# A batched attention and gated FFN layer on one core: a second buffer for the gated product, smaller units of work, and the order of an iteration as one table

## The chip, the cores and the metric

One core of a Trainium2 chip runs the whole kernel. The metric is the device time of one execution in microseconds. The engines are PE (TensorE: matmuls, with its weight loads shown apart as PEld), ACT (ScalarE), DVE (VectorE), POOL (GpSimd) and SP, which here only issues DMAs. Each engine works through its own list of instructions in order; semaphores tie the lists together.

## The reference

For 16 sequences x of 512 tokens and 256 channels (all fp32):

```
x  = layernorm(x + attention(x))          # 16 heads of 16, causal softmax, bqkv and bout
h  = silu(x W1 * s1) * (x W2 * s2)        # 256 -> 1024, gate and up
h  = gelu(h H1 * sh1); h = gelu(h H2 * sh2)   # 1024 -> 1024, twice, exact gelu
out = layernorm(x + (h W3) * s3)          # 1024 -> 256
```

## The kernel before, in words

**Stages.** Sequences are pipelined over 19 iterations (-1 to 17). Iteration i computes the attention of sequence i, prepares that of i+1, and does the feed-forward part of sequence i-1 and what is left of i-2. Each step in the list of an iteration carries that offset (0, 1, -1, -2). Iterations 3 to 14 run in a loop of two and hold every step; the first and the last iterations hold only those whose sequence exists. All engines walk the same list of steps and do their own part of each step, so the order of the list is the order of every engine's work. `plan_iteration` writes it: four blocks of exponentials (one for each group of four heads), each followed by one hidden layer over 256 tokens (a half) of the feed-forward part, whose eight column blocks are its units.

**Attention.** For key block kt (of 128) of a group, `exp` makes the scores of a pair of heads on PE into one of two PSUM banks `pS` (L834, L840), ACT takes the exponential into `probs_a` or `probs_b` (L530, L541), POOL masks the diagonal block of each pair (L488), and `pv` multiplies with the values (L873). ACT instructions per group: 4 + 4 single heads for kt 0 and 1, 2 pairs for kt 2, one of all four heads for kt 3, 11 in all. In the list one `exp` step stands for a pair of heads. `max` makes the row maxima of the group to come, two heads to a step (PE L851 into two banks `pM`, DVE L674), `neg_max` turns and stores them (DVE L682 and L684, PE L859, ACT L546, four DMAs of SP L416). `qk` projects queries and keys (PE L882, ACT `c_hi` L551, DVE `c_lo` L689), then SP saves them with five DMAs (L394).

**Feed-forward.** Operands are split into a high and a low part, so every product takes two matmuls. One `gu` unit is eight matmuls of 256 columns (L923), then

```
ACT  th[j%2] = tanh(gate)            L586
DVE  th[j%2] = (th[j%2] + 1) * up    L703
DVE  th[j%2] = gate * s2 * th[j%2]   L706
ACT  Xhi[j]  = th[j%2]               L592   (step ffn_hi)
POOL Xlo[j]  = th[j%2] - Xhi[j]      L494   (step ffn_hi)
```

The two buffers of `th` are held until POOL has read them: the tanh of unit j waits for the Xlo of unit j-2. The hidden layers take 16 matmuls per unit (L937); ACT writes the high part and the full value (L609, L610), DVE the low part (L714). The first unit of layer h1 waits for seven of the eight Xlo before its first matmul, for the eighth before its last pair. `ffn_out` (L950) and `y` (L904) are steps of both 128-token tiles of a half.

**Shared memory.** qk, v, gu, h1, h2, ffn_out, y, x1_turn, neg_max and den_turn share three PSUM banks in turn (`ring`); a step waits until the last user of its bank has been read. `th` lies over `Osb`, the attention's output row, so the ACT copy L571 waits for the feed-forward half before. A `table` step makes ACT load the table of Exp or Gelu (L597).

Of the kernel before, what the change touches and what calls it, by code (L numbers as in the profile page):

```python
# [55 lines left out]

def plan_iteration():

    steps = []

    def add(kind, off, *args):
        steps.append((kind, off, args))

    def exps(g, between):

        e = 0
        for kt in range(TB):  # L70
            for p in range(PAIRS):
                add("exp", 0, g, kt, p)
                steps.extend(between.get(e, []))
                e += 1
            if kt:
                add("pv", 0, g, kt - 1)

    def last_pv(g):
        add("pv", 0, g, TB - 1)
        add("o_out", 0, g)  # L80
        add("stack", 0 if g + 2 < NG else 1, (g + 2) % NG)

    def hidden(layer, off, half, g, early, after):

        if not early:
            last_pv(g)
            steps.extend(after.get(-1, []))
        for j in range(early, KB):  # L90
            add(layer, off, half, j)
            waiting = [(layer, half, k) for k in range(early)] if j == early else []
            for k, unit in enumerate(waiting):
                steps.append(("h_act", off, unit))
                if k == 0:
                    last_pv(g)
            if waiting:
                steps.append(("h_rest", off, waiting.pop(0)))
            add("h_act", off, layer, half, j)
            steps.extend(after.get(j, []))  # L100
            steps.extend(("h_rest", off, unit) for unit in waiting)
            add("h_rest", off, layer, half, j)

    def maxes(off, g):
        return [("max", off, (g, t, p)) for t in reversed(range(TB)) for p in range(PAIRS)]

    def gated(off, half, at, others):

        between = {e: list(more) for e, more in others.items()}
        for e, n in at:  # L110
            between.setdefault(e, []).append(("gu", off, (half, n)))
            if n:
                between.setdefault(e + (e == 6 and n == KB - 1), []).append(("ffn_hi", off, (half, n - 1)))
        return between


    m = maxes(0, 1)
    add("table", 0, "Exp", 0)
    exps(0, {0: [("y", -1, (0,)), m[0]], 1: [("y", -1, (1,))], 2: [("h2", -2, (1, 0))],
             4: [m[1]], 5: [m[2]], 6: [("h2", -2, (1, 1))], 7: [("ln1_stats", -1, ()), m[3]]})  # L120
    add("table", 0, "Gelu", 1)
    hidden("h2", -2, 1, 0, 2, {2: [m[4]], 3: [m[5]], 4: [m[6]], 5: [m[7]], 6: [("neg_max", 0, (1,))]})
    add("table", 0, "Exp", 2)
    add("ffn_out", -2, 1)
    m = maxes(0, 2)
    add("ln1", -1)

    exps(1, gated(-1, 0, [(4, 0), (4, 1), (5, 2), (5, 3), (6, 4), (6, 5), (7, 6), (7, 7)],
                  {0: [("qk", 0, (3,)), ("load_xT", 1, ()), m[0]], 1: [("x1_turn", -1, (0,))],
                   2: [("x1_turn", -1, (1,))], 3: [m[1]], 5: [m[2]]}))  # L130
    steps.append(m[3])
    add("ffn_hi", -1, 0, KB - 1)
    add("table", 0, "Gelu", 3)
    hidden("h1", -1, 0, 1, 0, {0: [m[4]], 1: [m[5]], 2: [m[6]], 3: [m[7]],
                               4: [("neg_max", 0, (2,))], 5: [("ln2_stats", -2, (1,))], 6: [("ln2", -2, (1,))]})

    m = maxes(0, 3)
    add("table", 0, "Exp", 4)
    add("qk", 1, 0)
    exps(2, {0: [("h2", -1, (0, 0))], 1: [m[0]], 2: [("h2", -1, (0, 1))], 3: [m[1]], 4: [m[2]], 6: [m[3]]})  # L140
    add("table", 0, "Gelu", 5)
    hidden("h2", -1, 0, 2, 2, {2: [m[4], ("load_x", 0, ())], 3: [m[5]], 4: [m[6]], 5: [m[7]], 6: [("neg_max", 0, (3,))]})
    add("table", 0, "Exp", 6)
    add("qk", 1, 1)
    add("ffn_out", -1, 0)
    m = maxes(1, 0)

    add("gu", -1, 1, 0)
    exps(3, gated(-1, 1, [(0, 1), (1, 2), (2, 3), (3, 4), (4, 5), (5, 6), (6, 7)],
                  {1: [m[0]]}))  # L150
    steps.append(m[1])
    add("ffn_hi", -1, 1, KB - 1)
    add("table", 0, "Gelu", 7)
    hidden("h1", -1, 1, 3, 0, {-1: [("v", 1, (0,)), m[2]], 0: [m[3], ("v", 1, (1,)), ("den", 0, ())],
                               1: [m[4], ("v", 1, (2,))], 2: [m[5], ("v", 1, (3,))], 3: [m[6], ("rec_save", 0, ())],
                               4: [m[7], ("rec_load", 0, ())], 5: [("neg_max", 1, (0,)), ("qk", 1, (2,))],
                               6: [("ln2_stats", -1, (0,)), ("den_turn", 0, ())], 7: [("ln2", -1, (0,))]})
    return steps
# [866 lines left out]
```

## Time and profile before

| | before |
|---|---|
| median of 3 runs | 2489.56 us (2488.16 to 2493.21) |
| the profiled execution: its time | 2490.49 us |
| its span, first to last instruction | 2488.7 us |
| PE busy | 2284.1 us, 92% |
| ACT busy, DVE busy | 1308.9 us, 1274.0 us |
| mean granted clock of PE | 0.961 |
| iterations -1 and 0 | from 18.2 to 194.2 us |
| iterations 1, 2 | start at 194.2, 334.4 us |
| iterations 3 to 14 | 478.8 to 2208.7 us, 144.2 us each |
| iterations 15, 16, 17 | start at 2208.7, 2346.9, 2462.3 us |

How to read it: an iteration starts with the first matmul of its first `exp` step (L834). A matmul's record holds its passage through the array as well, so records of matmuls that follow each other overlap; idle time is counted only where no record runs. "[0.54 <-DVE mx L674]" behind a row says that the engine was idle for 0.54 us before it and what ended the wait.

### The profile page before, as it was taken

The page shows a single profiled execution, that of the slowest core. Times are in us where ns is not written, and L with a number is a line of the kernel's source. Part 1 is how long each engine was busy: PE and PEld are TensorE (multiplying, and loading weights), DVE is VectorE, ACT ScalarE, POOL GpSimd, SP SyncE. Part 2 cuts the span into 40 slices and gives each one's busy share as a digit, 9 for nine tenths or more (in the row PEclk, how much of TensorE's full clock was granted, in tenths as well). Part 3 has the DMA queues.
Part 4 walks back from the last instruction along what each step waited for, and adds up shares of the span by engine and source line. Part 5 has one row for each costly group of instructions (what it writes and reads, how often), then busy time and mean ns, then how long its engine had stood idle before and what let it go on. Part 6 is the DMA issues. An engine that isn't in the chain of part 4 may idle for free. (4 is left out here: it accounts for less than half of the span.)

```text
span 2488.7 us, 51639 instructions
## 1 busy us (share of the span) xinstructions
PE 2284.1 (92%) x16294; PEld 1888.8 (76%) x16294; DVE 1274.0 (51%) x3963; ACT 1308.9 (53%) x2784; POOL 478.9 (19%) x894
## 2 busy tenths in 40 slices
PE   4566999999999999999999999999999999999987
PEld 2224888788788877878887787878778787887887
DVE  3364455555555455555545555554555555555433
ACT  1324555555565555556555555655555565655533
POOL 0112212212221221222122122211222121212211
PEclk8667999999999999999999999999999999999989
DMA  4851222122122212212221222222122222221000
GB/s 140 287 200 54 73 65 81 53 78 70 55 78 79 69 51 77 78 53 73 78 76 45 76 81 61 72 69 78 50 68 81 61 78 61 78 60 39 20 5 9
DMA packets 110394, 184.04 MB, mean 74 GB/s; under 512 B 21632, under 2 KB 39808, under 8 KB 109952
## 3 DMA queue, kind: packets, MB, share of 16 engines
q1 hardware_dynamic: 110128, 180.70, 25.3%
q8 instruction: 142, 2.33, 0.4%
q14 instruction: 124, 1.02, 0.1%
HBM read 109.86 MB, written 72.88 MB: 73 GB/s over the span
## 5 line engine op out<-in xcount | busy, mean ns | idle before, releaser
L674 DVE CUSTOM_DVE_ANT_0 pM<-pM,mask 128x512 f32<-128x512 f32 (+3 forms) x1024 | 490.4, 510 | 417.8 <-PE pM L851 340.7
L937 PE MATMUL ring<-Xhi,H 128*128 128x256 f32 x2048 | 538.3, 300 | 49.6 <-POOL Xlo L494 41.9
L937 PE MATMUL ring<-Xlo,H 128*128 128x256 f32 x2048 | 516.7, 289 | 0.0
L937 PE MATMUL ring<-Yhi,H 128*128 128x256 f32 x2048 | 509.2, 287 | 0.0
L937 PE MATMUL ring<-Ylo,H 128*128 128x256 f32 x2048 | 500.2, 282 | 0.0
L937 PEld LDWEIGHTS ring<-Xhi,H 128*128 128x128 f32 x2048 | 405.2, 198 | 65.9 <-POOL Xlo L494 30.0
L937 PEld LDWEIGHTS ring<-Xlo,H 128*128 128x128 f32 x2048 | 406.2, 198 | 4.4 <-issue 3.3
L937 PEld LDWEIGHTS ring<-Yhi,H 128*128 128x128 f32 x2048 | 390.6, 191 | 21.9 <-issue 21.2
L937 PEld LDWEIGHTS ring<-Ylo,H 128*128 128x128 f32 x2048 | 391.4, 191 | 0.7
L851 PE MATMUL pM<-Ks,Qs 128*128 128x512 f32 (+3 forms) x1024 | 285.8, 356 | 36.2 <-DVE mx L674 24.0
L609 ACT ACTIVATE Yhi<-ring,cols 128x256 fp32r<-128x256 f32 x256 | 121.6, 475 | 348.2 <-PE ring L937 309.8
L923 PE MATMUL ring<-x1Thi,W 128*128 128x256 f32 x1024 | 259.5, 288 | 9.2 <-DVE th L706 7.7
L851 PEld LDWEIGHTS pM<-Ks,Qs 128*128 128x128 f32 x1024 | 178.2, 196 | 105.5 <-DVE mx L674 58.2
L923 PE MATMUL ring<-x1Tlo,W 128*128 128x256 f32 x1024 | 254.2, 283 | 0.0
L488 POOL TENSOR_SCALAR_AFFINE_SELECT probs_a<-probs_a 128x256 f32<-128x256 f32 x256 | 104.3, 407 | 776.2 <-ACT probs_a L530 702.3
L610 ACT ACTIVATE full_h<-ring,cols 128x256 f32<-128x256 f32 x512 | 239.0, 467 | 0.0
L834 PE MATMUL pS<-Qs,Ks 128*128 128x512 f32 (+1 forms) x512 | 191.3, 431 | 39.5 <-DMA Qs<-nm 24.8
L494 POOL TENSOR_TENSOR Xlo<-th,Xhi 128x256 fp32r<-128x256 f32 x256 | 186.9, 733 | 210.1 <-ACT Xhi L592 210.1
L714 DVE TENSOR_TENSOR Xlo<-full_h,Xhi 128x256 fp32r<-128x256 f32 x256 | 109.7, 429 | 219.9 <-ACT full_h L610 217.4
L923 PEld LDWEIGHTS ring<-x1Thi,W 128*128 128x128 f32 x1024 | 195.2, 191 | 33.9 <-issue 17.3
L586 ACT ACTIVATE th<-ring,cols 128x256 f32<-128x256 f32 x256 | 121.6, 475 | 185.5 <-POOL Xlo L494 94.1
L609 ACT ACTIVATE Xhi<-ring,cols 128x256 fp32r<-128x256 f32 x256 | 120.7, 472 | 171.3 <-PE ring L937 123.3
(97 smaller groups left out, 3456.1 us busy)
## 6 DMA issues: line engine op xcount, KB each, us to landing
Qs<-qk_d SPq DMA_DIRECT2D x128, 256.0 KB, 3.9
Ks<-qk_d SPq DMA_DIRECT2D x64, 512.0 KB, 4.9
qk_d<-c_hi SPq DMA_DIRECT2D x64, 256.0 KB, 2.4
qk_d<-c_hi SPq DMA_DIRECT2D x128, 128.0 KB, 2.4
qk_d<-c_lo SPq DMA_DIRECT2D x128, 128.0 KB, 2.4
xTs<-in_xT SPq DMA_DIRECT2D x16, 512.0 KB, 4.0
Oc<-Osb SPq DMA_DIRECT2D x256, 32.0 KB
H<-raw SPq DMA_DIRECT2D x8, 1024.0 KB, 10.4
```

Of the source, the lines that this page charges most:

```text
L488: nc.gpsimd.affine_select(out=tri_p, in_=tri_p, compare_op=ALU.is_ge, fill=0.0, base=0, pattern=[[0, 2], [1, P]], channel_multiplier=-1).t ...
L494: nc.gpsimd.tensor_tensor(Xlo[:, j], th[:, j % 2], Xhi[:, j].bitcast(F32), ALU.subtract).then_inc(x_lo, 1)
L586: nc.scalar.activation(th[:, j % 2], ring[:, BANKS[kind, off, a], 0:HALF], ACT.Tanh, scale=s1_c[:, j:j + 1]).then_inc(tanh_done, 1)
L609: nc.scalar.activation(hi, src, ACT.Gelu, scale=sc)
L610: nc.scalar.activation(full_h[:], src, ACT.Gelu, scale=sc).then_inc(h_full, 1)
L674: nc.vector.tensor_tensor_reduce(pM[:, s, 0:n], pM[:, s, 0:n], mask[:, T - n:T], 1.0, NEG, ALU.add, ALU.max, mx[:, t, 2 * p + s:2 * p + s ...
L714: nc.vector.tensor_tensor(lo, full_h[:], hi.bitcast(F32), ALU.subtract).then_inc(h_lo, 1)
L834: nc.tensor.matmul(pS[:, u % 2, 0:n], keys[p], Qs[:, slot, p, s, kt * P:T], start=True, stop=True).then_inc(e_ready, 1)
L851: nc.tensor.matmul(pM[:, s, 0:n], Qs[:, slot, p, s, t * P:(t + 1) * P], Ks[:, slot, p, 0:n], start=True, stop=True).then_inc(m_ready, 1)
L923: mm = nc.tensor.matmul(to[:, n * HALF:(n + 1) * HALF], w, x_part, start=(c == 0 and X is x1Thi), stop=(c == CB - 1 and X is x1Tlo))
L937: mm = nc.tensor.matmul(to, w, x_part, start=(k == 0 and m == 0), stop=(k == KB - 1 and m == 1))
```

## The change

1. The second DVE operation of a gated unit writes a new pair of buffers, `full_g`, which ACT's copy and POOL's subtraction then read. `th` is free again when DVE has read it. `full_g` is laid over `c_hi`, the buffer of the qk step, and this brings two waits: DVE's second operation of the first unit of each half waits until SP's saves of the qk step before it have landed (`qk_saved`), and ACT's `c_hi` waits for the Xlo of the gated units before it.
2. Steps get smaller: one `exp` step is one of the 11 exponentials, one `max` step one head, a unit of h1 or h2 two steps of 8 matmuls each, `y` and `ffn_out` one tile each. The instructions stay the same in number and size.
3. The waits of PE for the low parts get finer: the first h1 or h2 unit starts when four of eight are there, then asks for six, seven and eight; `ffn_out` asks for all but four, then for all but one, then all.
4. `plan_iteration` reads the order from a table. In it, units 0 and 1 of the next group's exponentials stand before more other work, maxima stand apart, `ln1` stands before `ffn_out`, one `v` step before the last two `pv` of group 3, `qk:1:2` after the last h1 unit instead of before the seventh.

The table for the stretches that the prediction speaks of (a word is kind:offset:arguments), and the core of the rest:

```diff
+exp:0:0:0 exp:0:0:1
+
+table:0:Exp:0 y:-1:0:0 y:-1:0:1 max:0:1:3:0 y:-1:1:0 max:0:1:3:1 exp:0:0:2 exp:0:0:3 h2:-2:1:0:0 y:-1:1:1
+exp:0:0:4 exp:0:0:5 h2:-2:1:0:1 exp:0:0:6 exp:0:0:7 pv:0:0:0 exp:0:0:8 max:0:1:3:2 max:0:1:3:3 exp:0:0:9
+h2:-2:1:1:0 exp:0:0:10 max:0:1:2:0 h2:-2:1:1:1 max:0:1:2:1 pv:0:0:1 ln1_stats:-1 max:0:1:2:2 max:0:1:2:3
...
+table:0:Exp:2 ln1:-1 ffn_out:-2:1:0 ffn_out:-2:1:1 exp:0:1:0 exp:0:1:1 qk:0:3 load_xT:1 max:0:2:3:0 exp:0:1:2
+max:0:2:3:1 exp:0:1:3 x1_turn:-1:0 exp:0:1:4 x1_turn:-1:1 exp:0:1:5 pv:0:1:0 exp:0:1:6 exp:0:1:7 max:0:2:3:2
+max:0:2:3:3 gu:-1:0:0 gu:-1:0:1 ffn_hi:-1:0:0 exp:0:1:8 exp:0:1:9 max:0:2:2:0 gu:-1:0:2 ffn_hi:-1:0:1
+gu:-1:0:3 ffn_hi:-1:0:2 ffn_hi:-1:0:3 gu:-1:0:4 max:0:2:2:1 gu:-1:0:5 ffn_hi:-1:0:4 pv:0:1:1 exp:0:1:10
+gu:-1:0:6 ffn_hi:-1:0:5 gu:-1:0:7 ffn_hi:-1:0:6 pv:0:1:2 max:0:2:2:2 max:0:2:2:3 ffn_hi:-1:0:7
+
+table:0:Gelu:3 pv:0:1:3 o_out:0:1 stack:0:3 h1:-1:0:0:0 h1:-1:0:0:1 h_act:-1:h1:0:0 max:0:2:1:0 max:0:2:1:1
...
+h_rest:-1:h2:0:7 qk:1:1
+
+table:0:Exp:6 ffn_out:-1:0:0 ffn_out:-1:0:1 gu:-1:1:0 exp:0:3:0 exp:0:3:1 gu:-1:1:1 ffn_hi:-1:1:0 exp:0:3:2
...
+ffn_hi:-1:1:5 gu:-1:1:7 ffn_hi:-1:1:6 pv:0:3:1 exp:0:3:10 max:1:0:3:2 max:1:0:3:3 ffn_hi:-1:1:7 v:1:0 pv:0:3:2
+
+table:0:Gelu:7 pv:0:3:3 o_out:0:3 stack:1:1 max:1:0:2:0 max:1:0:2:1 h1:-1:1:0:0 h1:-1:1:0:1 h_act:-1:h1:1:0
...
+h_act:-1:h1:1:6 den_turn:0 h_rest:-1:h1:1:6 ln2_stats:-1:0 h1:-1:1:7:0 h_act:-1:h1:1:7 h_rest:-1:h1:1:7
+h1:-1:1:7:1 ln2:-1:0 qk:1:2
...
+        c_at = nc.sbuf_base
         c_hi = sb("c_hi", [P, T], F32R)
+        full_g = over(nc, c_at, "full_g", [P, 2, HALF], F32)
...
-                        nc.gpsimd.tensor_tensor(Xlo[:, j], th[:, j % 2], Xhi[:, j].bitcast(F32),
+                        nc.gpsimd.tensor_tensor(Xlo[:, j], full_g[:, j % 2], Xhi[:, j].bitcast(F32),
...
                         need(act, qk_saved, (b * NG + g) * SAVES)
+                        need(act, x_lo, (b - off - 1) * (2 * KB) + gated_before(g))
...
-                            need(act, x_lo, (b - 1) * (2 * KB) + (g + 1) // 2 * KB)
+                            need(act, ffn_full, (b - 1) * (2 * KB) + (g + 1) // 2 * KB)
...
-                        need(act, x_lo, b * (2 * KB) + n - 1)
+                        need(act, ffn_full, b * (2 * KB) + n - 1)
...
-                        nc.scalar.activation(Xhi[:, j], th[:, j % 2], ACT.Copy).then_inc(x_hi, 1)
+                        nc.scalar.activation(Xhi[:, j], full_g[:, j % 2], ACT.Copy).then_inc(x_hi, 1)
...
-                        nc.vector.scalar_tensor_tensor(out=th[:, j % 2], in0=gate,
+                        if j == 0:
+                            saved = (b + 2) * NG + qk_before(half)
+                            dve.wait_ge(qk_saved, (min(saved, B * NG) if isinstance(b, int) else saved) * SAVES)
+                        need(dve, x_lo, n - 1)
+                        nc.vector.scalar_tensor_tensor(out=full_g[:, j % 2], in0=gate,
...
-                        for k in range(KB):
-                            if j == 0 and k in (0, KB - 1):
-                                pe.wait_ge(s, n - (k == 0))
+                        for k in range(part * KB // 2, (part + 1) * KB // 2):
+                            if j == 0 and k in (0, KB // 2, KB - 2, KB - 1):
+                                pe.wait_ge(s, n - {0: 4, 4: 2, 6: 1, 7: 0}[k])
```

## Rows read from the trace of the kernel before

**Rows 1.** Part 1 of the page: busy time of each engine, share of the span.
```profile
PE 2284.1 (92%) x16294; PEld 1888.8 (76%) x16294; DVE 1274.0 (51%) x3963; ACT 1308.9 (53%) x2784; POOL 478.9 (19%) x894
```
**Rows 2.** Windows, one per iteration; length, busy of each engine, clock, DMA.
```profile
622.10:765.00 142.90, 137.96 (x1020) 115.34 (x1019) 77.07 (x247) 81.55 (x174) 29.57 (x55) 1.00 0.25 70
...
1198.70:1344.20 145.50, 140.55 (x1020) 117.94 (x1019) 77.09 (x247) 81.59 (x174) 29.55 (x55) 0.98 0.24 68
...
sum 1729.90, PE 1669.40 PEld 1396.94 DVE 925.73 ACT 978.95 POOL 354.73; mean PE 139.12 PEld 116.41 DVE 77.14 ACT 81.58 POOL 29.56
```
**Rows 3.** Window of iteration 8 behind the longest wait of PE.
```profile
1252.70:1259.50 6.80, 5.87 (x27) 5.87 (x28) 2.91 (x11) 3.29 (x7) 1.46 (x2) 0.50 0.09 19
```
**Rows 4.** Waits of the whole span: us in total, times, longest.
```profile
ACT th L586 <- POOL Xlo L494: 94.1, 141, 0.9
...
PEld pS L840 <- ACT probs_b L530: 54.1, 63, 1.4
PE ring L937 <- POOL Xlo L494: 41.9, 18, 4.0
```
**Rows 5.** Timeline of the gated stretch of iteration 8, ACT, DVE and POOL.
```profile
1250.32 0.47 ACT L586 ACTIVATE th<-ring,cols 128x256 f32<-128x256 f32 x1 [0.42 <-POOL Xlo L494]
...
1252.00 0.47 ACT L586 ACTIVATE th<-ring,cols 128x256 f32<-128x256 f32 x1 [0.90 <-POOL Xlo L494]
...
1252.96 0.48 DVE L706 SCALAR_TENSOR_TENSOR th<-ring,cols,th 128x256 f32<-128x256 f32 x1
...
1253.48 0.42 ACT L592 ACTIVATE Xhi<-th 128x256 fp32r<-128x256 f32 x1 [0.70 <-DVE th L706]
...
1253.97 0.73 POOL L494 TENSOR_TENSOR Xlo<-th,Xhi 128x256 fp32r<-128x256 f32 x1 [0.40 <-ACT Xhi L592]
```
**Rows 6.** Timeline of PE, same stretch: waits, and two neighbouring matmuls.
```profile
1248.44 0.39 PE L923 MATMUL ring<-x1Thi,W 128*128 128x256 f32 x1 [0.22 <-DVE th L706]
...
1250.99 0.41 PE L873 MATMUL pO<-probs_b,Vo 128*17 128x128 f32 x8 [0.24 <-POOL probs_b L488]
1253.63 0.58 PE L937 MATMUL ring<-Xhi,H 128*128 128x256 f32 x1 [2.22 <-POOL Xlo L494]
...
1260.74 0.28 PE L937 MATMUL ring<-Xlo,H 128*128 128x256 f32 x1
1260.86 0.28 PE L937 MATMUL ring<-Xhi,H 128*128 128x256 f32 x1
```
**Rows 7.** Timeline of PE in groups 0 and 3 of iteration 8.
```profile
1201.77 0.98 PE L834 MATMUL pS<-Qs,Ks 128*128 128x512 f32 x2 [0.26 <-ACT probs_a L530]
1202.59 1.89 PE L904 MATMUL ring<-Wout,Oc 128*128 128x256 f32 x8
...
1209.75 0.44 PE L851 MATMUL pM<-Ks,Qs 128*128 128x384 f32 x1 [0.54 <-DVE mx L674]
1210.39 0.44 PE L851 MATMUL pM<-Ks,Qs 128*128 128x384 f32 x1 [0.21 <-DVE mx L674]
...
1320.13 0.41 PE L873 MATMUL pO<-probs_b,Vo 128*17 128x128 f32 x8 [0.82 <-POOL probs_b L488]
```
**Rows 8.** Chain of waits: a gated unit, a hidden unit, one behind a pv.
```profile
2251.14 0.96 PE ring L923 x8
...
2296.24 2.10 PE ring L937 x16
2299.12 1.91 PE ring L937 x16
```
**Rows 9.** SP's queue in iteration 8: the first and last saves of a qk step.
```profile
1303.15 0.90 SPq L394 DMA_DIRECT2D qk_d<-c_hi  x2
...
1305.37 0.60 SPq L394 DMA_DIRECT2D qk_d<-c_hi  x1
```
**Rows 10.** Part 6 of the page: a save's time from issue to landing.
```profile
qk_d<-c_hi SPq DMA_DIRECT2D x64, 256.0 KB, 2.4
```
**Rows 11.** Windows of the two gated stretches of iteration 16.
```profile
2376.00:2394.93 18.93, 13.53 (x81) 12.83 (x81) 7.25 (x16) 6.36 (x16) 5.82 (x8) 0.77 0.00 1
2428.11:2445.74 17.63, 12.06 (x83) 11.36 (x82) 8.68 (x19) 6.47 (x16) 5.81 (x8) 0.85 0.00 1
```

More of the change, by code:

```diff
@@ L54 @@
 MISC = 3
-def plan_iteration():
[L62 to L158, printed above, removed]
@@ new lines, with value @@
+h_rest:-1:h1:1:3 h1:-1:1:4:0 h1:-1:1:4:1 h_act:-1:h1:1:4 max:1:0:0:2 max:1:0:0:3 rec_load:0 h_rest:-1:h1:1:4
+h1:-1:1:5:0 h1:-1:1:5:1 h_act:-1:h1:1:5 neg_split:1:0 neg_max:1:0 h_rest:-1:h1:1:5 h1:-1:1:6:0 h1:-1:1:6:1
+h_act:-1:h1:1:6 den_turn:0 h_rest:-1:h1:1:6 ln2_stats:-1:0 h1:-1:1:7:0 h_act:-1:h1:1:7 h_rest:-1:h1:1:7
+h1:-1:1:7:1 ln2:-1:0 qk:1:2
+"""
+def plan_iteration():
+    def value(word):
+        return int(word) if word.lstrip("-").isdigit() else word
+    steps = [[value(w) for w in entry.split(":")] for entry in ORDER.split()]
+    return [(s[0], s[1], tuple(s[2:])) for s in steps]
@@ L161, with bank_of @@
 STEPS = plan_iteration()
-BANKED = [s for s in STEPS if s[0] in
-          ("qk", "v", "gu", "h1", "h2", "ffn_out", "y", "x1_turn", "neg_max")]
+PARTED = {"h1": 2, "h2": 2, "ffn_out": 1, "y": 1}
+def bank_of(kind, off, args):
+    return (kind, off, args[:PARTED[kind]]) if kind in PARTED else (kind, off, args)
 def ring_banks():
@@ L170, in ring_banks, with qk_before, gated_before @@
     for kind, off, args in STEPS:
-        n = 2 if kind == "den_turn" else 1 if (kind, off, args) in BANKED else 0
-        for m in range(n):
-            key = (kind, off, args + (m,)) if kind == "den_turn" else (kind, off, args)
-            banks[key] = at % MISC
-            at += 1
+        if kind == "den_turn":
+            keys = [(kind, off, (m,)) for m in range(CB)]
+        elif kind in ("qk", "v", "gu", "x1_turn", "neg_max") or kind in PARTED:
+            keys = [bank_of(kind, off, args)]
+        else:
+            keys = []
+        for key in keys:
+            if key not in banks:
+                banks[key] = at % MISC
+                at += 1
     return banks
 BANKS = ring_banks()
+def qk_before(half):
+    first = next(n for n, s in enumerate(STEPS) if s[0] == "gu" and s[2][0] == half)
+    return sum(s[0] == "qk" for s in STEPS[:first]) - sum(s[0] == "qk" and s[1] == 0 for s in STEPS)
+def gated_before(g):
+    at = next(n for n, s in enumerate(STEPS) if s[0] == "qk" and s[2] == (g,))
+    return sum(s[0] == "ffn_hi" for s in STEPS[:at])
 def steps_of(i):
@@ L727, in work @@
                                                     ALU.mult).then_inc(o_norm, 1)
-                    elif kind == "y":
-                        half, = a
+                    elif kind == "y" and a[1]:
+                        half, _ = a
                         xr = xz[:, (odd + off) % 2]
@@ L754, in work @@
                         row.then_inc(ln1, 1)
-                    elif kind == "ffn_out":
-                        half, = a
+                    elif kind == "ffn_out" and a[1]:
+                        half, _ = a
                         at = b * LN2 + 6 * half
-                        f = ring[:, BANKS[kind, off, a]].rearrange("p (t c) -> p t c", c=C)
+                        f = ring[:, BANKS[bank_of(kind, off, a)]].rearrange("p (t c) -> p t c", c=C)
                         two = xz[:, (odd + off) % 2, 2 * half:2 * half + 2]
@@ L806, in iteration, with bank @@
             def iteration(i, steps, odd, taken, general):
-                def bank(kind, off, a):
+                def bank(kind, off, a, first=True):
                     n = BANKS[kind, off, a]
+                    if not first:
+                        return ring[:, n]
                     if n in taken:
@@ new lines, in iteration @@
+                        for p in sorted({p for p, _ in heads}):
+                            wide = [k for k, (m, _) in enumerate(heads) if m == p]
+                            first, last = heads[wide[0]][1], heads[wide[-1]][1]
+                            mm = nc.tensor.matmul(pS[:, nth % 2, n * wide[0]:n * (wide[-1] + 1)],
+                                                  Ks[:, slot, p, kt * P:(kt + 1) * P],
+                                                  Qs[:, slot, p, first:last + 1, kt * P:T], start=True, stop=True)
```

191 lines of the change are left out of this document (105 added, 86 removed).

## The prediction

> **What bounds the kernel now.** I read the page's busy times, then the windows by iteration, the waits, and the timeline of one iteration. PE is busy 92% of the span and no other engine over 53% [rows 1], so the time is PE's work, plus what PE waits, plus what its clock takes. The twelve full iterations take 1729.9 us, 144.2 each [rows 2]. The view has twelve such rows: six at granted clock 1.00 with a mean length of 143.1 us (622.10:765.00 stands for them), six at 0.98 or 0.99 and up to 145.9 (1198.70:1344.20 stands for them). So about 1.0 us an iteration is lost to the clock. In iteration 8 all of it lies in one stretch at 0.50, the lower of its two levels, and that stretch begins inside PE's longest wait [rows 3, 6].
>
> In iteration 8 PE sits idle for 145.5 - 140.55 = 4.95 us [rows 2]. That is a lower bound of its waits: a matmul's record lasts 0.28 us where the next one starts 0.12 us later [rows 6], so each wait hides 0.16 us or more under the record before it. There are some fifteen such places, so the waits come to 5.0 + 15 x 0.16 = 7.4 us. Starts against starts of unhindered steps of the same kind (a gated unit 0.96, a hidden unit 1.91 [rows 8]) give about the same, 7.5. The rest, 135.6 us, is work that the change keeps.
>
> Where they are. (A) The gated stretch of group 1, before h1: 0.22 + 0.24 + 2.22 us idle [rows 6], 3.3 with what is hidden. The cause is a loop across three engines: ACT's list has tanh(j), then the copy of unit j-1; POOL subtracts; then only is `th` free for tanh(j+1). Tanh starts are 1252.00 - 1250.32 = 1.68 us apart [rows 5], against PE's 0.96 [rows 8]; ACT waits so 141 times, 94.1 us [rows 4]. PE's units pile up behind it and h1 waits for the last low parts. (B) The last `pv` of group 3: 0.82 idle [rows 7], 1.0 in all; its mask stands behind late subtractions on POOL. (C) The exponentials of group 0: 0.26 + 0.54 + 0.21 idle [rows 7], 1.7 in all; a pair of heads is asked for while ACT and DVE have just begun the pair before. (D) The same in groups 1 to 3, seen only in the weight loads (54.1 us for one form [rows 4]), some 1.6 us an iteration.
>
> **The change, part by part.**
> *Two more buffers.* `th` is now held from the tanh to the end of DVE's second operation, 1252.96 + 0.48 - 1252.00 = 1.44 us; `full_g` from 1252.96 to POOL's end at 1253.97 + 0.73, 1.74 us [rows 5]. With two of each that is 0.72 and 0.87 us a unit, under PE's 0.96. PE sets the pace again. The last unit's chain from its tanh to Xlo stays: 1253.97 + 0.73 - 1252.00 = 2.7 us [rows 5]. After the last gated unit (1248.44 + 0.96 + its wait, so 1249.6) PE has a `pv`, two maxima and a `pv`, which end at 1250.99 + 0.41 [rows 6], 1.8 us with their wait and 1.4 without, and now also seven eighths of the first h1 unit, 1.7 [rows 8]: 3.1 us against 2.7 and ACT's queue of two or three instructions in front of that chain. I leave 0.7 us of wait of the 3.3: A gives 2.6.
> *B.* The exponential of kt 3 stands before two maxima, the `v` step and a `pv`, and POOL no longer lags: 1.0 gained. `v` before the last two `pv` makes ACT's copy to `Vo` wait for the last `pv`, with the table load and the output copy queued behind it; the h1 unit in between (1.9 us [rows 8]) covers them, so nothing. Without that cover it would cost about 1.3.
> *Single exp and max steps.* They cost no instruction. In group 0 there now stand three of the four tiles of `y` and two maxima between exponentials 1 and 2; two tiles last 1.89 us with their passage [rows 7], so some 2.5 us, in which ACT gets through both. I take 1.6 of C's 1.7. For D, I take 0.7 of 1.6: in groups 1 and 3 ACT has exponentials, tanh and copies together, and its in-order queue will still make PE wait.
> *Half units.* The cost of a split is bounded by 0 and by the difference of two hidden units, 2.10 behind a `pv` against 1.91 [rows 8]; I take 0, as no fp32 step stands between most halves. Three such neighbourhoods vanish (two pairs of `pv` become adjacent, `v` joins them) and `y` adds one: two times 0.19, 0.3 gained.
> *`ln1` before `ffn_out`* on DVE fills time in which it waited for PE: nothing alone, it is in D. *`qk:1:2` behind the last h1 unit* puts ACT's c_hi before the exponentials of group 0; exponential 2 has the 2.5 us of cover above: nothing. ACT's new wait of c_hi for the Xlo: h1 has used them all by then, nothing. ACT's copy to `Osb` now waits for DVE instead of POOL, which comes earlier: nothing. SP's list keeps its DMAs and nearly its order, with the saves of `qk:1:2` a unit later; nobody waits for these before the next block.
> *New waits.* DVE's second operation of a half's first unit waits for the saves. From the first issue at 1303.15 to the last at about 1305.4, and 2.4 us to land [rows 9, 10]: 4.6 us behind c_lo. In half 1, `ffn_out` (32 matmuls at 0.12, 3.8 us) and the first gated unit stand between, so the saves land at about the same moment as they are asked for; in half 0 it is six exponentials, both `x1_turn`, a `pv`, two maxima and a gated unit, an estimated 5 us or more. Bounds: 0, and two waits of 1.5. Behind that operation stand DVE's maxima and the release of the gated unit's bank, so PE would feel it one to one. I take 0.2 an iteration, and 0.4 for finer handoffs that don't fit.
> Sum of waits: 2.6 + 1.0 + 1.6 + 0.7 + 0.3 - 0.6 = 5.6 us. *Clock:* the fall follows the 2.22 us wait; with 0.7 left I expect it to go, 1.0 us. Together 6.6 us an iteration.
>
> The clock is the place where I weigh a rule. The rows show one fall, right at the one long wait [rows 3, 6], but six iterations with the same wait have none [rows 2]. The Trainium skill, page "TensorE: Matmul & The Clock Gate", section "A second HAM failure mode: psum-queue depth-cycling", says that many small idle moments between groups of matmuls while cycling through PSUM banks can make the gate go up and down. By it the falls would stay, as small waits stay, and the sum would be 5.6.
>
> **Outside the loop.** Iteration 1 lacks some steps: 5 us. Iterations 2 to 15 as above: 14 x 6.6 = 92. In iteration 16 the gated stretches up to the end of the first h1 unit take 18.9 and 17.6 us [rows 11]. Now: eight units (7.7, and an estimated 1.9 more in the first at the low clock that shows in the 0.77), 2.7 of chain, 0.3 of last matmuls: 12.6 and 10.7. That is 6.3 + 6.9, and an estimated 1.8 of low clock behind them: 15 us. Up to 194 us DMAs and weight tests rule; 0, within 5 either way. Sum: 5 + 92 + 15 = 112. The profiled execution took 2490.5 us, 0.9 over the median; 2490.5 - 112 - 0.9 = 2377.
>
> **The rivals.**
> 1. *The waits go elsewhere.* With the `th` loop gone, ACT (81.6 of 144 us busy, crowded in the gated blocks) or the three ring banks bind, or the falls of the clock stay. For it: D's waits, and the rule above. Against: ACT's pitch there is 0.8 us a unit by its two durations less their overlap [rows 5]. Only A and the tail: 15 x 2.6 + 15 = 54, 2436; falls alone staying, 2377 + 14 = 2391.
> 2. *More than I give.* All 7.5 and the clock: 15 x 8.8 + 18 = 150, 2340.
> 3. *Slower: the saves bind.* Place: the second operation of the first unit of each half, behind SP's queue [rows 9, 10]. SP issues in order; if a transfer with a wait stood ahead of the saves, they'd come late. The point from which it decides is where the two waits together pass 6.6 us an iteration, that is landings 8 us behind c_lo instead of 4.6. At 9 us: 2 x 4.3 = 8.6 lost, net 2.0 x 15 - 15 = 15 us slower, 2505. Against: the steps that SP has ahead are done long before in this trace.
> 4. *The table does not change PE's order much*, since PE's records show 92% busy: within 0.2% (about 5 us, what a measurement can tell from no change). Against: the 94.1 us of ACT's waits [rows 4].
>
> **How the numbers follow.** Forecast, 2355 to 2405 (the falls staying included): 0.58. Rival 1 beyond that: 0.25. Rival 2: 0.11. Rival 3: 0.04. Rival 4: 0.02. Faster by over 0.2% then 0.94, same 0.02, slower 0.04. The range runs from rival 2's value to just short of rival 1's, 2342 to 2430, with about 2 in 10 left outside.
>
> **What would show it.** Right: ACT th waiting for DVE th or PE and no more for POOL; tanh starts about 1.0 us apart in iteration 16; PE's wait before h1 under 0.8 us and POOL probs_b gone from PE's waits; windows of 137 to 138 us at clock 1.00. Wrong: windows above 140 us; DVE's second gated operation idle behind SP's saves; PE's waits for ACT probs_a or probs_b grown; falls to 0.50 in the same place with no long wait ahead.

## The result, and the profile after

The changed kernel takes 2341.3 us (median of 4 runs, 2337.4 to 2344.8) where the kernel before takes 2491.3 on the same chip: ratio 0.940, 95% interval 0.938 to 0.942. I had said 2377. The side and the mechanisms were right, the size was not: 150 us came off, 112 were forecast, and the result lies just under the range (its lower end is 2342), beside the value of rival 2. The span of the profiled execution went from 2488.7 to 2335.7 us.

Part 1 of the page of the changed kernel, and from part 2 the granted clock in 40 slices:

```profile
PE 2208.9 (95%) x16294; PEld 1869.4 (80%) x16294; DVE 1277.3 (55%) x3963; ACT 1308.2 (56%) x2784; POOL 476.3 (20%) x894
...
PEclk8667999999999999999999999999999999999999
```

The counts are those of [rows 1], and DVE, ACT and POOL do the same work in the same time. Nothing was saved in work: PE is the engine whose time fell, as it waits less. PE's own figure falls too, since a matmul's record that was stretched, by a wait inside a step or by the low clock, is short again.

Windows of two iterations and of the twelve together (3 to 14):

```profile
1001.00:1136.80 135.80, 134.70 (x1021) 115.71 (x1019) 77.37 (x247) 81.50 (x174) 29.47 (x55) 1.00 0.26 73
1136.80:1271.60 134.80, 134.36 (x1019) 115.73 (x1018) 77.32 (x247) 81.49 (x174) 29.37 (x55) 1.00 0.26 73
...
460.60:2082.20 1621.60, 1614.65 (x12219) 1388.93 (x12217) 928.72 (x2953) 977.74 (x2088) 352.60 (x660) 1.00 0.26 73
```

1621.6 / 12 = 135.1 us an iteration against 144.2 [rows 2]. In iteration 8 PE is idle for 134.80 - 134.36 = 0.44 us, where it was 4.95, and the clock is 1.00 in all of them; from 223 us to the last 4 us of this execution it never falls. The 153 us between the two spans divide into: up to iteration 1, 1.6 (forecast 0); iteration 1, 6.9 (forecast 5); iterations 2 to 15, 126.7 or 9.05 each (forecast 92, 6.6 each); iterations 16 and 17, 17.9 (forecast 15). That is 41 us more than the forecast's sum of 112. The medians lie 150 us apart, as the profiled execution of the changed kernel is 3.9 us below its median.

Waits over the whole span; the lines L578, L532, L701 and L929 are L586, L530/L541, L706 and L937 of before:

```profile
ACT th L578 <- PE ring L915: 70.1, 80, 4.0
...
PEld pS L831 <- ACT probs_b L532: 41.0, 53, 0.9
...
DVE full_g L701 <- DMA qk_d<-c_hi: 8.5, 16, 1.1
...
PE ring L929 <- POOL Xlo L490: 1.0, 3, 0.4
```

ACT's 141 waits for POOL before a tanh, 94.1 us [rows 4], are gone: the view has no such row any more, and what ends ACT's wait there is PE. PE's wait before h1 went from 41.9 us [rows 4] to 1.0. DVE's wait for the saves came as forecast, at "about the same moment as they are asked for": 16 times, 0.53 us on average, one an iteration.

The end of the gated stretch of iteration 8, ACT, DVE and POOL, beside [rows 5]:

```profile
1184.77 0.48 ACT L578 ACTIVATE th<-ring,cols 128x256 f32<-128x256 f32 x1
...
1185.78 0.48 DVE L701 SCALAR_TENSOR_TENSOR full_g<-ring,cols,th 128x256 f32<-128x256 f32 x1
...
1186.30 0.42 ACT L584 ACTIVATE Xhi<-full_g 128x256 fp32r<-128x256 f32 x1 [0.58 <-DVE full_g L701]
...
1186.79 0.74 POOL L490 TENSOR_TENSOR Xlo<-full_g,Xhi 128x256 fp32r<-128x256 f32 x1 [0.27 <-ACT Xhi L584]
```

And PE in the same stretch, beside [rows 6] (the last row is the first matmul of the pair that waits for the last Xlo):

```profile
1184.66 0.63 PE L864 MATMUL pO<-probs_a,Vo 128*17 128x256 f32 x8
1185.22 0.61 PE L842 MATMUL pM<-Ks,Qs 128*128 128x384 f32 x2
1185.76 0.41 PE L864 MATMUL pO<-probs_b,Vo 128*17 128x128 f32 x8
1186.11 0.39 PE L929 MATMUL ring<-Xhi,H 128*128 128x256 f32 x1
...
1187.88 0.28 PE L929 MATMUL ring<-Xhi,H 128*128 128x256 f32 x1
```

The chain of the last unit is what I gave it: 1186.79 + 0.74 - 1184.77 = 2.76 us (2.7 forecast). But ACT's queue delays that tanh by 0.1 us at most, as it starts 0.1 us after PE has gone on to the `pv` behind the unit, and its Xlo is there at 1187.53, 0.35 us before the last pair of the h1 unit begins. No row of PE carries a wait. The 2.22 us of [rows 6] are gone entirely.

Iteration 16, where no attention work covers anything: two tanh starts, then the windows that answer to [rows 11].

```profile
2240.61 0.47 ACT L578 ACTIVATE th<-ring,cols 128x256 f32<-128x256 f32 x1 [0.48 <-PE ring L915]
2241.57 0.48 ACT L578 ACTIVATE th<-ring,cols 128x256 f32<-128x256 f32 x1
```

```profile
2238.40:2250.23 11.83, 10.57 (x80) 9.91 (x81) 7.14 (x16) 6.82 (x16) 5.90 (x8) 1.00 0.00 1
2282.87:2294.61 11.74, 10.32 (x83) 9.74 (x81) 8.58 (x19) 6.82 (x16) 5.91 (x8) 1.00 0.01 1
```

Tanh starts are 0.96 us apart, PE's own pace, where the loop across three engines had set 1.68 [rows 5]. The stretches take 11.8 and 11.7 us (forecast 12.6 and 10.7, before 18.9 and 17.6), at clock 1.00 where it was 0.77 and 0.85.

Just ahead of the first of them PE waits for the layernorm `ln1` before it can turn x1. The row of before, then the one that is left:

```profile
2372.62 1.11 PE L912 MATMUL ring<-ident,xz 128*128 128x128 f32 x4 [2.87 <-DVE xz L752]
```

```profile
2236.36 0.63 PE L904 MATMUL ring<-ident,xz 128*128 128x128 f32 x4 [1.24 <-DVE xz L760]
```

With `ln1` before `ffn_out` in the list, DVE writes `xz` while PE still works on `ffn_out`, and the first `x1_turn` (2234.52 us) no longer waits. The second waits 1.24 us for its bank.

### The profile page after: what moved, and what is told of

It reads as the page before. It is cut to its first block and busy times, and to the rows that moved or that the text cites. A ratio compares the mean times of both kernels' runs of the same rounds, so it can differ in the third digit from the quotient of the medians.

```text
span 2335.7 us, 52022 instructions
## 1 busy us (share of the span) xinstructions
PE 2208.9 (95%) x16294; PEld 1869.4 (80%) x16294; DVE 1277.3 (55%) x3963; ACT 1308.2 (56%) x2784; POOL 476.3 (20%) x894
## 5 line engine op out<-in xcount | busy, mean ns | idle before, releaser
L929 PE MATMUL ring<-Xhi,H 128*128 128x256 f32 x2048 | 515.4, 291 | 6.6 <-ACT full_h L602 5.0
L929 PE MATMUL ring<-Yhi,H 128*128 128x256 f32 x2048 | 507.3, 285 | 0.0
L929 PE MATMUL ring<-Ylo,H 128*128 128x256 f32 x2048 | 502.6, 282 | 0.0
L929 PE MATMUL ring<-Xlo,H 128*128 128x256 f32 x2048 | 499.2, 282 | 0.0
L929 PEld LDWEIGHTS ring<-Xhi,H 128*128 128x128 f32 x2048 | 391.0, 191 | 18.7 <-ACT full_h L602 11.7
L929 PEld LDWEIGHTS ring<-Ylo,H 128*128 128x128 f32 x2048 | 390.8, 191 | 3.2
L929 PEld LDWEIGHTS ring<-Xlo,H 128*128 128x128 f32 x2048 | 392.0, 191 | 1.1
L929 PEld LDWEIGHTS ring<-Yhi,H 128*128 128x128 f32 x2048 | 390.2, 191 | 2.6
L842 PE MATMUL pM<-Ks,Qs 128*128 128x512 f32 (+3 forms) x1024 | 302.1, 355 | 32.6 <-DVE mx L665 17.0
L831 PE MATMUL pS<-Qs,Ks 128*128 128x512 f32 (+2 forms) x768 | 267.9, 409 | 31.2 <-DMA Qs<-nm 23.6
L532 ACT ACTIVATE probs_a<-pS 128x512 f32<-128x512 f32 x384 | 210.7, 592 | 106.8 <-PE pS L831 105.1
L831 PEld LDWEIGHTS pS<-Qs,Ks 128*128 128x128 f32 x768 | 137.7, 194 | 138.4 <-issue 47.4
L532 ACT ACTIVATE probs_b<-pS 128x384 f32<-128x384 f32 (+1 forms) x320 | 154.2, 513 | 116.6 <-PE pS L831 74.6
L490 POOL TENSOR_TENSOR Xlo<-full_g,Xhi 128x256 fp32r<-128x256 f32 x256 | 187.8, 736 | 151.2 <-ACT Xhi L584 146.5
```

The lines of the kernel that those rows point to most:

```text
L490: nc.gpsimd.tensor_tensor(Xlo[:, j], full_g[:, j % 2], Xhi[:, j].bitcast(F32), ALU.subtract).then_inc(x_lo, 1)
L532: nc.scalar.activation(dst, src, ACT.Exp, scale=SCALE).then_inc(exp_done, 1)
L831: mm = nc.tensor.matmul(pS[:, nth % 2, n * wide[0]:n * (wide[-1] + 1)], Ks[:, slot, p, kt * P:(kt + 1) * P], Qs[:, slot, p, first:last + 1 ...
L842: nc.tensor.matmul(pM[:, h % 2, 0:n], Qs[:, slot, h // 2, h % 2, t * P:(t + 1) * P], Ks[:, slot, h // 2, 0:n], start=True, stop=True).then ...
L929: mm = nc.tensor.matmul(to, w, x_part, start=(k == 0 and m == 0), stop=(k == KB - 1 and m == 1))
```

## The experiments

"Starts against starts" means here: the time from a step's first matmul to the next step's, less what the same kind of step takes unhindered, summed over an iteration. It holds the waits, what they hide, the clock, and small fixed costs between steps. Per iteration, by halves of the four groups (an Exp block and the Gelu block behind it; before and e1 have `qk:1:2` inside the last, the others at its end, which moves some 0.4 us from there into the first). The level of these figures depends on which step is taken as unhindered; the differences between the rows do not:

```
                 group 0       group 1       group 2       group 3
               Exp0  Gelu1   Exp2  Gelu3   Exp4  Gelu5   Exp6  Gelu7    sum
before         3.46   0.59   3.33   3.74   1.74   0.59   2.70   1.93   18.1
e1_old_order   3.47   0.59   2.56   0.43   1.72   0.58   2.59   1.99   13.9
e2_one_pair    1.57   0.46   2.16   1.92   1.40   0.38   2.46   1.45   11.8
changed        1.57   0.46   2.03   0.43   1.40   0.38   1.35   1.39    9.0
```

Theory 1 was mine: two separate gains, the `th` loop with its fall of the clock, and the order with its small steps. The rivals: that the order alone is small, that the saves of `c_hi` or the finer waits matter, that the half units are only a cost, that the clock does not hang on the long wait.

**e1_old_order: two buffers and the finer waits, in the order of before.** The table is written so that every engine has the old order, pairs of exponentials and maxima and whole units included:

```diff
-table:0:Exp:0 y:-1:0:0 y:-1:0:1 max:0:1:3:0 y:-1:1:0 max:0:1:3:1 exp:0:0:2 exp:0:0:3 h2:-2:1:0:0 y:-1:1:1
+table:0:Exp:0 exp:0:0:0 exp:0:0:1 y:-1:0:0 y:-1:0:1 max:0:1:3:0 max:0:1:3:1 exp:0:0:2 exp:0:0:3 y:-1:1:0
+y:-1:1:1 exp:0:0:4 exp:0:0:5 h2:-2:1:0:0 h2:-2:1:0:1 exp:0:0:6 exp:0:0:7 pv:0:0:0 exp:0:0:8 max:0:1:3:2
...
```

> The changed kernel (two full_g buffers, finer waits for the low parts) with the order of before written in the new table: pairs of exponentials and of maxima, both halves of a hidden unit side by side, qk:1:2 before the seventh h1 unit. Theory 1 (the order and the buffers each remove their own waits, and the clock falls only behind a long wait of PE): the wait before h1 goes, iterations 144.2 - 2.8 - 1.0 = 140.3 us at clock 1.00, total about 2420, ratio 0.971. Theory 2 (falls of the clock come from many small waits, which this order keeps): falls to 0.50 stay, iterations 141.4, total about 2435. Theory 3 (the order does nearly all; the th loop was hidden): total 2470 or more.

2413.0 us, ratio 0.969 (0.968 to 0.971). Window of iterations 3 to 14, and PE's waits in it:

```profile
470.40:2149.90 1679.50, 1653.05 (x12219) 1384.28 (x12218) 925.14 (x2952) 974.06 (x2088) 354.69 (x660) 1.00 0.26 71
```

```profile
PE pM L843 <- DVE mx L666: 9.0, 24, 0.5
PE ring L930 <- ACT full_h L603: 6.5, 12, 0.7
PE pO L865 <- POOL probs_b L485: 6.4, 12, 0.5
PE pS L832 <- ACT probs_a L533: 3.1, 12, 0.3
```

139.96 us an iteration, 4.2 less than before. No row of PE waiting for Xlo is left in these iterations even in the old order, and the falls of the clock are gone with it. Gelu3 gives 3.3 and Exp2 0.8 of the 4.2; 1.0 of that is the clock. So the waits of A came to 3.1 us, of which I had given 2.6. This run has the finer waits as well as the buffers; no run has the finer waits alone in the old order, so how the 3.1 us divide between the two is not shown there.

**e2_one_pair: the new table, `th` written in place as before.**

```diff
-                        nc.vector.scalar_tensor_tensor(out=full_g[:, j % 2], in0=gate,
+                        nc.vector.scalar_tensor_tensor(out=th[:, j % 2], in0=gate,
...
-                        need(act, ffn_full, b * (2 * KB) + n - 1)
+                        need(act, x_lo, b * (2 * KB) + n - 1)
```

> The new table, but the gated product stays in th as before (no full_g, the tanh of unit j waits for the Xlo of unit j-2, no wait for the saves). Theory 1: the loop of 1.68 us a unit is back in both halves, PE waits about 2.5 to 3 us in half 0 and about 1.5 in half 1, and the clock falls again in some iterations: iterations about 140.5 us, total about 2430, ratio 0.976. Theory 3 (the order does nearly all): iterations under 137, total under 2370.

2390.5 us, ratio 0.961 (0.959 to 0.963), 40 us under what my theory gave. The window, and PE's two largest waits in it:

```profile
465.40:2120.50 1655.10, 1627.01 (x12219) 1390.79 (x12217) 928.72 (x2953) 975.83 (x2088) 352.15 (x660) 1.00 0.26 72
```

```profile
PE ring L924 <- POOL Xlo L490: 11.5, 24, 0.6
PE pO L859 <- POOL probs_b L484: 8.6, 12, 0.7
```

137.9 us an iteration. The `th` loop is back, over the whole span:

```profile
ACT th L577 <- POOL Xlo L490: 62.6, 87, 0.9
```

It costs 2.8 us against the changed kernel (Gelu3 1.5, Exp6 1.1), but here it reaches PE as two waits of 0.6 us or less, and the clock does not fall. The finer waits, which this run has too, may have a share in that; it is not shown apart. Buffers and order overlap: one without the other they give 4.2 (e1) and 6.2, together 9.0. The 1.0 of the clock is in both. POOL's late masks (B) also need both changes: 12 waits of `pv` for probs_b are left in e1 (0.5 us each) and in e2 (0.7), none in the changed kernel.

**e3_coarse_waits: the changed kernel with the two waits of before** (seven of eight low parts, then all).

```diff
-                            if j == 0 and k in (0, KB // 2, KB - 2, KB - 1):
-                                pe.wait_ge(s, n - {0: 4, 4: 2, 6: 1, 7: 0}[k])
+                            if j == 0 and k in (0, KB - 1):
+                                pe.wait_ge(s, n - (k == 0))
```

> The changed kernel with the coarse waits for low parts of before (first hidden unit: seven of eight ahead of its first matmul, the eighth ahead of its last pair; ffn_out likewise). Theory 1: the chain behind the last gated unit is 2.7 us and PE has 1.4 us of other work ahead of h1, so without the finer waits h1:0 starts some 0.8 us later in half 0 and little later in half 1; iterations 135.9 to 136.4, total 2353 to 2363, of it up to 2 us in iterations 16 and 17. Rival (the finer waits do nothing, the chain is over in time): total within 3 us of the changed kernel's 2341.

2353.4 us, ratio 0.945 (0.944 to 0.947), 135.7 us an iteration. PE's first wait in iterations 3 to 14:

```profile
PE ring L929 <- POOL Xlo L490: 4.8, 12, 0.4
```

0.4 us once an iteration, 0.47 from start to start. The other 0.14 of the 0.6 us comes in the last Gelu block, where no row shows a wait. So with coarse waits about the 0.7 us that I had left standing of A does appear; the finer waits, with the cover that I had counted (3.1 us, 3.2 measured), take it away.

**e4_over_Yhi: `full_g` laid over `Yhi`**, which is free then, so that neither DVE waits for the saves nor ACT's `c_hi` for Xlo.

```diff
+        y_at = nc.sbuf_base
         Yhi = sb("Yhi", [P, KB, HALF], F32R)
+        full_g = over(nc, y_at, "full_g", [P, 2, HALF], F32)
...
-                        if j == 0:
-                            saved = (b + 2) * NG + qk_before(half)
-                            dve.wait_ge(qk_saved, (min(saved, B * NG) if isinstance(b, int) else saved) * SAVES)
```

> The changed kernel with full_g laid over the first two blocks of Yhi, which are free in the gated stretches, instead of over c_hi: no wait of DVE for SP's saves and none of ACT's c_hi for the Xlo. Theory 1 (the wait for the saves, 0.53 us of DVE idle 16 times in the trace, is off PE's path): total within 3 us of the changed kernel. Rival (PE feels it through the release of the gated unit's bank one to one): 16 x 0.5 = 8 us less, 2333.

2344.6 us, ratio 0.942 (0.941 to 0.944), 3.3 us above the changed kernel's time on another chip, and 135.1 us an iteration, the changed kernel's to 0.05. In the loop the 0.53 us that DVE waits for the saves are on nobody's path. My 0.2 for them was 0, and rival 3 falls. (Outside it, iteration 15 of the profiled execution takes 135.8 us against 129.6; see the last section.)

**e7_whole_units: each second half of an h unit or `y` tile moved right behind the first.** In the table, for the first block:

```diff
-exp:0:0:4 exp:0:0:5 h2:-2:1:0:1 exp:0:0:6 exp:0:0:7 pv:0:0:0 exp:0:0:8 max:0:1:3:2 max:0:1:3:3 exp:0:0:9
...
+h2:-2:1:0:0 h2:-2:1:0:1 exp:0:0:4 exp:0:0:5 exp:0:0:6 exp:0:0:7 pv:0:0:0 exp:0:0:8 max:0:1:3:2 max:0:1:3:3
...
```

> The table of the changed kernel with the second half of each h1 and h2 unit moved right behind the first, and the second tile of y likewise; all else stays. Theory 1 (half units matter only where they stand between exponentials and maxima: some seven places an iteration, each with a handoff to ACT or DVE of 0.3 to 0.6 us no longer covered): 1 to 2 us an iteration more, total 2356 to 2372. Rival (the places don't matter, only how much work stands in a block): within 3 us of 2341.

2374.9 us, ratio 0.954 (0.952 to 0.955): 33 us slower than the changed kernel, more than I had given it. 137.5 us an iteration, with the largest wait

```profile
PE pS L831 <- ACT probs_b L532: 9.7, 24, 0.4
```

where the changed kernel has no such row in these iterations. With the half unit gone from between them, four exponentials stand in a row, and in groups 0 and 2 the seventh comes 0.56 us later, the next two 0.2 and 0.1 more: 1.7 us in all. Two maxima of group 0 and one of the last Gelu block cost the other 0.5. The rejoined tiles of `y` cost nothing: 0.19 us more behind the first, 0.19 less behind exponential 4. So 2.3 of the 4.9 us that order and small steps bring hang on the half units of h1 and h2: they are filler of a fitting size. (The rest of the table was made for them; a table made for whole units might lose less. Not tried.)

**e8_pairs: exponentials and maxima in pairs again.**

```diff
-max:0:2:3:1 exp:0:1:3 x1_turn:-1:0 exp:0:1:4 x1_turn:-1:1 exp:0:1:5 pv:0:1:0 exp:0:1:6 exp:0:1:7 max:0:2:3:2
...
+max:0:2:3:1 exp:0:1:2 exp:0:1:3 x1_turn:-1:0 exp:0:1:4 exp:0:1:5 x1_turn:-1:1 pv:0:1:0 exp:0:1:6 exp:0:1:7
...
```

> The table of the changed kernel with the second exponential of each pair, and the second maximum, moved right behind the first. Most exponentials stand in pairs already, so this moves mostly maxima. Theory 1: two maxima in a row need two free pM banks, and DVE takes 0.85 us for a row of 512; a few places stall by 0.2 to 0.5 us: 0.5 to 1.2 us an iteration, total 2349 to 2359. Rival (maxima are covered anyway): within 3 us of 2341.

2348.2 us, ratio 0.943 (0.942 to 0.945), 135.7 an iteration. The single steps are worth 0.6 us an iteration, the half units four times that.

**e5_long_wait and e6_shorter_wait: a wait of PE made on purpose.** Coarse waits as in e3, and POOL does three more subtractions (one in e6) into `Ylo`, which nobody reads then, before the seventh Xlo of half 0. They add work and leave the output as it is.

```diff
+                        for m in range(3 if half == 0 and j == KB - 2 else 0):
+                            nc.gpsimd.tensor_tensor(Ylo[:, m], full_g[:, j % 2], Xhi[:, j].bitcast(F32), ALU.subtract)
```

> The kernel of the coarse waits with one long wait put back: before the seventh Xlo of half 0, POOL makes three more subtractions of 0.73 us into Ylo, which is free there. PE then waits 0.4 + 2.2 = 2.6 us ahead of the first h1 matmul of half 0 in each iteration, about as in the kernel before (2.2). Theory 1 (a fall of the clock to 0.50 follows a long wait of PE): falls of 3.4 to 7 us appear in about half of the iterations right behind that wait, as before; iterations 135.75 + 2.2 = 137.95 without and up to 140.8 with a fall, total 2353 + 33 + 15 = about 2400. Rival (the falls of before needed the many small waits as well): no fall between 230 us and the last iterations, total about 2386.

2398.9 us, ratio 0.964 (0.962 to 0.966). Two iterations of it, both with this wait (2.46 and 2.48 us), then the 3.4 us behind the second:

```profile
606.40:744.00 137.60, 134.65 (x1019) 115.74 (x1018) 77.26 (x247) 81.62 (x174) 31.46 (x58) 1.00 0.26 72
744.00:883.80 139.80, 136.31 (x1021) 117.25 (x1019) 77.37 (x247) 81.68 (x174) 31.46 (x58) 0.99 0.26 71
...
796.70:800.10 3.40, 3.40 (x19) 3.40 (x18) 0.28 (x1) 0.66 (x2) 0.03 (x1) 0.50 0.18 40
```

```profile
658.27 0.39 PE L931 MATMUL ring<-Xhi,H 128*128 128x256 f32 x1 [2.46 <-POOL Xlo L492]
...
796.09 0.39 PE L931 MATMUL ring<-Xhi,H 128*128 128x256 f32 x1 [2.48 <-POOL Xlo L492]
```

The falls are back, behind PE's long wait as in [rows 3], in 8 of the 12 iterations. These are 139.0 to 139.7 us long, against 137.6 of those with the same wait and no fall: 1.3 to 2.1 us each.

> As the run with the long wait, with one more subtraction of 0.73 us instead of three: PE waits 0.4 + 0.7 = 1.1 us ahead of h1 of half 0. Theory 1 (it takes a wait of about 2 us or more, since 0.96 us in the run with one pair of buffers had no fall in the full iterations): no fall in iterations 3 to 14, iterations 135.75 + 0.7 = 136.5, total about 2365. Rival (falls grow in number with the wait): some falls in these iterations, and up to 2372.

2366.4 us (one run, beside 2486.9 for the kernel before). The window and the wait:

```profile
465.00:2102.50 1637.50, 1616.07 (x12218) 1388.97 (x12217) 927.80 (x2953) 979.79 (x2088) 361.56 (x672) 1.00 0.26 73
```

```profile
PE ring L931 <- POOL Xlo L492: 13.1, 12, 1.1
```

Twelve waits of 1.1 us and not one fall. No run has a wait between 1.1 and 2.2 us in its loop (for iterations 15 and 16 see the last section), and nothing tells why of two iterations with the same wait one has the fall.

**e9_neighbours: like beside like.** Two `v` steps put behind two others, `pv:0:1:2` beside `pv:0:1:3`, to see whether the fixed 0.19 us behind such a step can be shared.

```diff
-gu:-1:0:6 ffn_hi:-1:0:5 gu:-1:0:7 ffn_hi:-1:0:6 pv:0:1:2 max:0:2:2:2 max:0:2:2:3 ffn_hi:-1:0:7
+gu:-1:0:6 ffn_hi:-1:0:5 gu:-1:0:7 ffn_hi:-1:0:6 max:0:2:2:2 max:0:2:2:3 ffn_hi:-1:0:7 pv:0:1:2
...
-max:1:0:2:2 max:1:0:2:3 v:1:1 den:0 h_rest:-1:h1:1:0 h1:-1:1:1:0 max:1:0:1:0 max:1:0:1:1 v:1:2
+max:1:0:2:2 max:1:0:2:3 den:0 h_rest:-1:h1:1:0 h1:-1:1:1:0 max:1:0:1:0 max:1:0:1:1 v:1:2 v:1:3
```

> The table of the changed kernel with three fp32 steps moved beside others of the kind: v:1:1 behind v:1:0, v:1:3 behind v:1:2, pv:0:1:2 beside pv:0:1:3. Theory 1 (each change between fp32 steps and the others costs PE about 0.1 to 0.19 us, which no engine's wait shows): three neighbourhoods less, 0.6 to 0.75 us an iteration, total 2341 - 10 = 2331, if the two Vo copies in a row on ACT ahead of the table load stay covered. Rival (no such cost, or the copies stall PE): 2341 or more.

2362.0 us, ratio 0.949 (0.947 to 0.950): slower than the changed kernel, a miss. PE's waits in iterations 3 to 14, and one of them:

```profile
PE ring L930 <- ACT full_h L603: 14.4, 24, 0.9
```

```profile
1129.90 0.39 PE L930 MATMUL ring<-Xhi,H 128*128 128x256 f32 x1 [0.93 <-ACT full_h L603]
```

The ring hands out its three banks in the order of the list; with two `v` before it, `h1:1:2` gets the bank of `h1:1:1` and waits for ACT to read it, 0.93 us. A `v` behind a `v` is held up too (0.86 against 0.67 us from start to start), so nothing is shared there. The two `pv` together do gain: 0.31 us, less 0.12 that return inside the first h1 unit, where it waits for the last Xlo (argued: no row shows so short a wait).

**e10_two_moves, e11_two_moves_Yhi, e12_changed_again.** What was good in e9 alone, and one maximum moved behind a `pv`, where PE had waited for DVE's maximum ahead of an exponential; the same with `Yhi`; and the changed kernel beside them.

```diff
-exp:0:2:8 max:0:3:2:1 exp:0:2:9 max:0:3:2:2 pv:0:2:1 max:0:3:2:3 exp:0:2:10 h2:-1:0:2:0 h2:-1:0:2:1
+exp:0:2:8 max:0:3:2:1 exp:0:2:9 pv:0:2:1 max:0:3:2:2 max:0:3:2:3 exp:0:2:10 h2:-1:0:2:0 h2:-1:0:2:1
```

> The changed kernel with two steps moved: pv:0:1:2 beside pv:0:1:3, and max:0:3:2:2 behind pv:0:2:1. From the run with neighbouring fp32 steps: the starts around pv:0:1:2 came 0.31 us closer and h1:0:0 then waited 0.12 for the Xlo, so 0.19 gained; two pv in a row save, a v beside a v does not. The maximum waits 0.14 to 0.3 us for DVE in its present place, which the pv covers: 0.2. Theory 1: 0.4 us an iteration, 6 us less than the changed kernel on the same chip. Rival (the wait moves to the next maximum, and h1 waits for the Xlo what the pv gained): within 2 us of it.

> The two moves and full_g over Yhi, so without the wait for the saves. Theory 1 (that wait is off the path): the same as with the two moves alone, within 2 us. Rival: up to 8 us less.

> The changed kernel itself once more, on the same chip as the two that follow, so that a few us can be told: 2341 within 4 us, ratio 0.940.

2331.7 us (ratio 0.937, 0.935 to 0.938), 2335.2 (0.937, 0.936 to 0.939) and 2343.4 (0.941, 0.939 to 0.942), five runs each. e10's window:

```profile
456.60:2071.80 1615.20, 1609.17 (x12219) 1389.85 (x12217) 927.94 (x2953) 977.84 (x2088) 352.54 (x660) 1.00 0.27 74
```

134.6 us an iteration, 0.5 less than the changed kernel's 135.1. e10 is faster than the changed kernel: its median is 11.8 us under e12's (6 forecast), and the two intervals do not meet. The twelve iterations give 5.7 of it, those before and behind them 4.0 (spans 2326.2 and 2335.9 us); the last 2 are the spread of single runs. Of the 4.0, 1.8 lie in iteration 15, where a maximum on DVE comes late in both (last section), so not all of the 11.8 belongs to the two moves. `Yhi` adds nothing that can be told: e11 lies 3.5 us above e10, with the same iterations in the loop.

## Why the prediction was right in kind and too small

**What bounds the kernel.** Right. PE sets the time, 7.5 us of waits and 1.0 of clock were there to be had, and the 135.6 us of kept work is about what an iteration now takes (135.1). The steps that failed are the shares of these waits that I left standing for ACT's queue (A and D), the half units taken at 0, and the 0.6 us set aside for new waits. They stand below one by one.

**A, 2.6 of 3.3 forecast, 3.1 measured (e1).** The loop across ACT, DVE and POOL was the cause, the hold times and the chain of 2.7 us were right. The step "I leave 0.7 us of wait" failed: it had two or three instructions of ACT delay the chain, and they delay it by 0.1 us at most; the chain is 2.76 us long and the cover with the finer waits 3.2. Where the waits are coarse, 0.6 us does appear (e3).

**B, 1.0 forecast.** Exp6 gives 1.24 (e1 against the changed kernel), right. It takes both changes (e1, e2).

**C, 1.6 forecast, 2.3 measured.** Exp0 falls by 1.9 with `qk:1:2`'s 0.4 moved into it. More than the whole 1.7 that I had seen in idle time went, so the idle rows of [rows 7] did not show all of it; a part is the vanished neighbourhood of a `pv`, which the forecast had apart.

**D, 0.7 of 1.6 forecast.** The other blocks give about 1.4 together (0.53, 0.32, 0.20, 0.13, and 0.20 of Gelu7 once the moved 0.4 is taken off). The step "its in-order queue will still make PE wait" failed: PE waits for probs_b no more in these iterations, and its weight loads wait for ACT's exponentials 3.1 us in iteration 8 where it was 6.4. Most exponentials now have work of another kind beside them. That this is the reason is argued; e8 and e7, where such work is taken away again, cost 0.6 and 2.3 us.

**Half units, taken at 0 with 0.3 for neighbours.** This is the step that went most astray in its reasoning. I bounded what a split costs and did not ask what it gives. Rejoined, the units cost 2.3 us an iteration (e7). C's cover had counted the `y` tiles and maxima alone; what was nowhere is the h2 half between exponentials 5 and 6 of groups 0 and 2, 0.87 us in each.

**New waits, -0.6 forecast, 0 measured.** The saves land as forecast but DVE has the time (e4), and finer handoffs fit.

So order and small steps brought 4.9 us where I had 3.0: B 0.2, C 0.7 and D 0.7 too low, 0.6 for new waits that did not come, and 0.3 for neighbours that these block figures hold already. With A's 0.5 that is the 2.4 us an iteration, 36 us over 15 iterations. Iteration 16 gave 18.0 against 15, of which the two gated stretches give 13.0 (13.2 forecast) and what lies around them 5.0 where I had an estimated 1.8 of low clock. Ahead of the first stretch 2.5 us went, and the step that failed there is "*`ln1` before `ffn_out`*: nothing alone": PE's wait of 2.87 us is down to 1.24. The low clock (0.94 in that part before, 1.00 now) can have given no more than the rest. Between the stretches 0.5 went, with a clock of 0.98 before. Behind the second 2.0 went: 1.0 by shorter waits for ring banks (1.9 us before, 0.9 now), and 0.7 in the one step at the low clock. The last 1.6 us, up to iteration 1, have no run that explains them.

**The clock, 1.0 forecast.** Right, 1.03. In iterations 3 to 14 the falls went, and they come back with a wait of 2.5 us (e5), not with 1.1 (e6), nor with e1's 60 waits of up to 0.7 us in twelve iterations. The rule from the Trainium skill that I weighed, page "TensorE: Matmul & The Clock Gate", section "A second HAM failure mode: psum-queue depth-cycling" (in a bf16 kernel that cycles through PSUM banks, many small idle moments between groups of matmuls make the gate go up and down), would have kept the falls in e1; the trace disagrees at this amount of idle time, 26 us idle of 1680 (its window above) and clock 1.00.

**The rivals.** Rival 1 (the waits go elsewhere) had 0.25 and none of it came. It rested on ACT's crowding in the gated blocks, but ACT is 60% busy over an iteration (81.5 of 135.1 us), and its tanh now keep PE's pace of 0.96 us. Rival 3 fell with e4. Rival 4 took PE's 92% for work, and its records stretch with its waits. Rival 2 is nearest, but not quite what happened: without the clock 8.0 us went, 0.5 more than the 7.5, and by its own terms (7.5 and 1.0) it gives 8.5 us an iteration and 2344, as its 8.8 holds the neighbours' 0.3 too. That its 2340 is so near is in part luck. It had 0.11 and should have had more: each "I leave" was a guess at the cautious side, and five of them in one direction are no longer a likeliest value.
